# Half-array first scores, x_lo last, and copies of batch 0 first in a gated attention kernel

## What is computed

```python
qp = einsum('oc,bcn->bon', Wq, instance_norm(layernorm(x))) + bq
kp = einsum('oc,bcm->bom', Wk, instance_norm(ctx)) + bk
sp = einsum('oc,bcm->bom', Ws, ctx) + bs
attn = softmax(einsum('bcn,bcm->bnm', qp, kp), axis=-1)
mean = einsum('bnm,bvm->bvn', attn, sp)
std = sqrt(relu(einsum('bnm,bvm->bvn', attn, sp * sp) - mean * mean))
x = x + tanh(g_xattn) * (instance_norm(ctx) * std + mean)
x = x + tanh(g_ffn) * (layernorm(x) @ w.T)
```

## Time and profile before

| | |
|---|---|
| median of 3 runs | 191.2 us (191.08 to 192.58) |
| the profiled execution: own time | 191.17 us |
| the profiled execution: span | 189.4 us |
| TensorE busy | 168.2 us (89% of the span) |
| VectorE busy | 140.7 us (74%) |
| GpSimd busy | 133.9 us (71%) |
| ScalarE busy | 131.8 us (70%) |
| DMA queue of SyncE, share of 16 engines | 37.0% |

### The profile page before, as it was taken

How to read it: one execution, slowest core, us unless ns; L and a number is a source line. 1 busy time by engine, 2 the same in 40 slices (tenths; PEclk the granted TensorE clock), 3 DMA queues, 4 the chain that set the end, 5 groups by cost and what they waited for, 6 DMA issues and landing times.

```text
span 189.4 us, 2916 instructions
## 1 busy us (share of the span) xinstructions
PE 168.2 (89%) x816; PEld 104.7 (55%) x816; DVE 140.7 (74%) x321; ACT 131.8 (70%) x283; POOL 133.9 (71%) x155
## 2 busy tenths in 40 slices
PE   0349699999999999989998999899979889999993
PEld 0325455665556466545654565456435444888881
DVE  3877798679976967997699769994896753585641
ACT  2365766949796879759786968697779689626210
POOL 2225578538995899679969987998979999494100
PEclk9999999999999999999999999999999999999999
DMA  6248491477068427813680470064000000021312
GB/s 188 82 96 236 110 239 44 116 172 268 2 141 262 154 49 173 294 42 88 165 294 12 105 175 0 0 157 123 3 2 0 0 0 3 5 106 55 114 55 111
DMA packets 10880, 20.09 MB, mean 106 GB/s; under 512 B 1648, under 2 KB 1776, under 8 KB 10864
## 3 DMA queue, kind: packets, MB, share of 16 engines
q1 hardware_dynamic: 10864, 19.90, 37.0%
HBM read 9.67 MB, written 2.10 MB: 62 GB/s over the span
## 4 chain that ended last, share of the span: by engine, by line
PE 64%; DVE 15%; POOL 5%; issue 4%; ACT 4%; DMA 3%; SPq 2%; DVEq 0%; POOLq 0%; ACTq 0%
PE pv_bank L364 19%; PE score_bank L340 10%; PE turn_bank L351 10%; DVE neg_max L694 4%; PE score_bank L397 4%; PE score_bank L401 4%; PE score_bank L398 4%; POOL probs L889 3%; PE proj_bank L376 3%; PE proj_bank L322 3%; DMA params_sb<-in_params 2%; POOL x_lo L882 2%; ACT probs L492 2%; PE score_bank L387 2%; SPq L249 2%
## 5 line engine op out<-in xcount | busy, mean ns | idle before, releaser
L889 POOL TENSOR_SCALAR probs<-probs,rden 128x512 f32<-128x512 f32 x64 | 55.0, 859 | 19.4 <-DVE rden L700 19.1
L492 ACT ACTIVATE probs<-score_bank,neg_max 128x512 f32<-128x512 f32 x64 | 44.5, 696 | 24.2 <-DVE neg_max L694 23.9
L364 PE MATMUL pv_bank<-probs_t,values 128*128 128x512 f32 x120 | 60.2, 604 | 0.9 <-ACT VAR L509 0.6
L694 DVE TENSOR_REDUCE neg_max<-score_bank 128x1 f32<-128x512 f32 x64 | 43.4, 680 | 18.9 <-PE score_bank L340 18.8
L351 PEld LDWEIGHTS turn_bank<-ident,probs 128*128 128x128 f32 x256 | 29.4, 141 | 27.0 <-issue 22.4
L351 PE MATMUL turn_bank<-ident,probs 128*128 128x128 f32 x256 | 37.1, 277 | 4.3 <-ACT probs_t L500 2.9
L500 ACT COPY probs_t<-turn_bank 128x512 f32<-128x512 f32 x64 | 37.9, 591 | 1.2 <-PE turn_bank L351 1.0
L364 PEld LDWEIGHTS pv_bank<-probs_t,values 128*128 128x128 f32 x120 | 19.7, 190 | 13.0 <-issue 12.5
L340 PE MATMUL score_bank<-k_hi,q_hi 64*128 64x512 f32 x32 | 16.3, 509 | 2.8 <-DVE k_lo_swapped L776 2.5
L340 PE MATMUL score_bank<-k_hi_swapped,q_hi_swapped 64*128 64x512 f32 x32 | 16.3, 509 | 0.0
L397 PE MATMUL score_bank<-w_hi,yt_hi 128*128 128x512 f32 x32 | 13.6, 424 | 0.0
(11 more groups left out here) (105 smaller groups left out, 340.2 us busy)
## 6 DMA issues: line engine op xcount, KB each, us to landing
X<-in_x SPq DMA_DIRECT2D x8, 256.0 KB, 3.0
CTX<-in_context SPq DMA_DIRECT2D x8, 256.0 KB, 3.7
q_hi_swapped<-q_hi SPq DMA_DIRECT2D x16, 128.0 KB, 2.3
q_lo_swapped<-q_lo SPq DMA_DIRECT2D x16, 128.0 KB, 2.4
ctx_now<-in_context SPq DMA_DIRECT2D x8, 256.0 KB, 2.7
sz<-in_scales_zeros SPq DMA_DIRECT2D x4, 512.0 KB, 5.1
out<-result SPq DMA_DIRECT2D x8, 256.0 KB, 2.0
k_hi_swapped<-k_hi SPq DMA_DIRECT2D x15, 128.0 KB, 2.4
```

The costliest lines, as they stand in the source:

```text
L364: mm = pe.matmul(sums_bank(t, b)[:, :], values[:, i, b, :, :].rearrange("p a c -> p (a c)"), probs_t[b][:, i, :], start=(i == 0), stop=(i ...
L492: act.activation(probs[c % SBANKS][:, :], score_bank[c % SBANKS][:, :], ACT.Exp, bias=neg_max[:, c:c + 1], accum_out=den[:, c:c + 1]).then ...
L694: dve.tensor_reduce(neg_max[:, c:c + 1], score_bank[c % SBANKS][:, :], AX_X, ALU.max, negate=True).then_inc(max_done, 1)
L889: pool.tensor_scalar(probs[c % SBANKS][:, :], probs[c % SBANKS][:, :], rden[:, c:c + 1], 1.0, ALU.mult, ALU.mult).then_inc(probs_done, 1)
```

## The change

Five edits. (1) `project` issues the two products that read the hi part first and waits for the lo part only before the third. (2) A new function `first_scores(c)` makes the chunks 0 to 3 of tile 0 one after the other on the lower half of the array, where batch 0 lies, from q and k themselves; the shifted copies of batch 0 of tile 0 fall away on SyncE (two), ScalarE (one) and VectorE (one), and the counts of `swapped[0][0]` and of the wait in `maximum` follow. (3) VectorE runs the statistics of tile 1 after `keep_lo` of tile 0 instead of before. (4) SyncE issues the four copies of batch 0 of the next tile as each of q_hi, q_lo, k_hi, k_lo is ready, and the four of batch 1 after them. (5) In the start the context tile for the values is loaded before x and context of tile 2.

```diff
--- before.py
+++ after.py
@@ -262,28 +262,27 @@
             load(1, *first_loaded[1])
 
             sp.wait_ge(q_hi_done, 1)
-            swap(0, 0, swap_q_hi)
+            swap(0, 1, swap_q_hi)
             sp.wait_ge(q_lo_done, 1)
-            swap(0, 0, swap_q_lo)
+            swap(0, 1, swap_q_lo)
             sp.wait_ge(k_lo_done, 1)
-            swap(0, 1, swap_q_hi, swap_q_lo, swap_k_hi, swap_k_lo)
+            swap(0, 1, swap_k_hi, swap_k_lo)
+            sp.dma_start(ctx_now[:, :], dram_tile(context_tiles, 0)).then_inc(ctx_now_loaded, DMA)
             load(2, *first_loaded[2])
-            sp.dma_start(ctx_now[:, :], dram_tile(context_tiles, 0)).then_inc(ctx_now_loaded, DMA)
 
             def body(t):
 
                 if not has_next(t):
                     return
                 sp.wait_ge(q_hi_done, t + 2)
+                swap(t + 1, 0, swap_q_hi)
                 sp.wait_ge(q_lo_done, t + 2)
-                for b in range(2):
-                    swap(t + 1, b, swap_q_hi, swap_q_lo)
+                swap(t + 1, 0, swap_q_lo)
                 sp.wait_ge(k_hi_done, t + 2)
-                for b in range(2):
-                    swap(t + 1, b, swap_k_hi)
+                swap(t + 1, 0, swap_k_hi)
                 sp.wait_ge(k_lo_done, t + 2)
-                for b in range(2):
-                    swap(t + 1, b, swap_k_lo)
+                swap(t + 1, 0, swap_k_lo)
+                swap(t + 1, 1, swap_q_hi, swap_q_lo, swap_k_hi, swap_k_lo)
                 sp.wait_ge(s_done, t + 1)
                 sp.dma_start(ctx_now[:, :], dram_tile(context_tiles, t + 1)).then_inc(ctx_now_loaded, DMA)
 
@@ -318,16 +317,27 @@
                     (x_hi, x_lo, x_hi_done, x_lo_done, q_done), (c_hi, c_lo, c_hi_done, c_lo_done, k_done))[which]
                 into = bank_of(t, which)
                 pe.wait_ge(hi_done, t + 1)
+                pe.matmul(into[:, :], w_qk_hi[:, which, :], hi[:, :], start=True, stop=False)
+                pe.matmul(into[:, :], w_qk_lo[:, which, :], hi[:, :], start=False, stop=False)
                 pe.wait_ge(lo_done, t + 1)
-                pe.matmul(into[:, :], w_qk_hi[:, which, :], hi[:, :], start=True, stop=False)
-                pe.matmul(into[:, :], w_qk_hi[:, which, :], lo[:, :], start=False, stop=False)
-                pe.matmul(into[:, :], w_qk_lo[:, which, :], hi[:, :], start=False, stop=True).then_inc(done, 1)
+                pe.matmul(into[:, :], w_qk_hi[:, which, :], lo[:, :], start=False, stop=True).then_inc(done, 1)
+
+            def first_scores(c):
+
+                rows = slice(0, C)
+                if c == 0:
+                    pe.wait_ge(q_lo_done, 1)
+                    pe.wait_ge(k_lo_done, 1)
+                for step, (q_part, k_part) in enumerate(((q_hi, k_hi), (q_lo, k_hi), (q_hi, k_lo))):
+                    mm = pe.matmul(score_bank[c][:, :], q_part[0][rows, P * c:P * c + P], k_part[0][rows, :],
+                                   start=(step == 0), stop=(step == 2))
+                mm.then_inc(scores_done, 1)
 
             def scores(t, c):
 
                 b, p = c // JC, t % 2
                 if c % JC == 0:
-                    pe.wait_ge(swapped[b][p], SWAP * (t // 2 + 1))
+                    pe.wait_ge(swapped[b][p], SWAP * (t // 2 + (0 if (b, p) == (0, 0) else 1)))
                     pe.wait_ge(k_lo_done, t + 1)
                 if not (is_first(t) and c < SBANKS):
                     pe.wait_ge(exp_done, CHUNKS * t + c + 2 - SBANKS)
@@ -405,9 +415,8 @@
             pe.wait_ge(w_split, 1)
             project(0, 0)
             project(0, 1)
-            for c in range(0, SBANKS, 2):
-                scores(0, c)
-            pe.wait_ge(q_lo_done, 1)
+            for c in range(SBANKS):
+                first_scores(c)
             project(1, 0)
             pe.wait_ge(ident_ready, 1)
 
@@ -549,8 +558,6 @@
                 act.copy(part[:, :], whole).then_inc(part_done, 1)
             keep_hi(0, 0)
             keep_hi(0, 1)
-            act.wait_ge(k_hi_done, 1)
-            act.copy(k_hi_swapped[0][C:P, :], k_hi[0][0:C, :].bitcast(F32)).then_inc(swapped[0][0], DMA)
             act.preload_act_table_set("natural_log_exp_and_others")
             for c in range(AHEAD_E):
                 exponentials(0, c)
@@ -690,7 +697,7 @@
 
             def maximum(t, c):
 
-                dve.wait_ge(scores_done, CHUNKS * t + 2 * (c // 2) + 2)
+                dve.wait_ge(scores_done, CHUNKS * t + (c if is_first(t) and c < SBANKS else 2 * (c // 2) + 1) + 1)
                 dve.tensor_reduce(neg_max[:, c:c + 1], score_bank[c % SBANKS][:, :], AX_X, ALU.max,
                                   negate=True).then_inc(max_done, 1)
 
@@ -769,11 +776,9 @@
             dve.wait_ge(c_hi_done, 1)
             dve.tensor_tensor(c_lo[:, :], tile_of(CTX, 0), c_hi[:, :].bitcast(F32),
                               ALU.subtract).then_inc(c_lo_done, 1)
-            statistics(1)
             keep_lo(0, 0)
             keep_lo(0, 1)
-            dve.wait_ge(k_lo_done, 1)
-            dve.tensor_copy(k_lo_swapped[0][C:P, :], k_lo[0][0:C, :].bitcast(F32)).then_inc(swapped[0][0], DMA)
+            statistics(1)
             normalise(1, 0)
             dve.wait_ge(gates_ready, 1)
             for c in range(AHEAD_S):
```

## The result

| | before | changed |
|---|---|---|
| median | 191.45 us (191.08 to 192.58, 4 runs) | 193.69 us (193.25 to 194.35, 4 runs) |
| ratio, 95% interval | | 1.0109 (1.0056 to 1.0163) |
| profiled execution: own time, span | 191.17, 189.4 us | 194.35, 192.5 us |
| mean granted clock of TensorE | 1.00 | 0.961 |

The change makes the kernel slower by about 1.1%; the forecast was 190.9 us, the range ended at 191.9. The profiled execution is the slowest of the four; the others took 193.25 to 193.82 us, with a mean granted clock of 0.997 to 1.00, and what follows is read from the profiled one.

The account below looks back on a forecast made before the run. Bound by a sequence across all engines until 30 us, TensorE alone in tiles 1 and 2, then a VectorE-TensorE loop. Only the start's 0.25 us counted: 191.17 - 0.25 = 190.92, forecast 190.9 us, range 189.5 to 191.9.

Parts of the forecast that it names:

- First projection product: Tile 0: no longer waiting for x_lo, it starts at 6.84 instead of 7.75; the projections end 0.91 us earlier.
- first score product: Tile 0: without waiting for shifted copies it starts at 11.4 instead of 13.11, 1.7 us earlier.
- first maximum: Tile 0 on VectorE: starts between 14.9 and 15.0, where it stood (14.89).
- the moved statistics pay back a gain: Start, VectorE: tile 1's statistics behind k_lo pay back the projections' 0.9 us and the scores' 1.7 us.
- x_lo on GpSimd was covered: Tile 1: x_lo moves to about 15.1 to 16.4, its projection ends near 17, before q_hi at 17.89; cost nothing.
- The scores of tile 1 are released by no copy: Tile 1: scores start after the transposes at about 25.75 instead of 26.11, with 0.07 about 0.45 us sooner.
- Tiles 3 to 5: About 0.48 us of each x projection's wait is filled, but q_lo comes no sooner; gain taken as 0.
- rival A: Tiles 3 to 5: the x projection's 0.48 us counts three times, 1.44 us in all; time 189.5; chance 0.15.
- the last step of the sum: Tile 1: GpSimd's squared values limit the first weighing, 27.15 instead of 27.39; 0.24 of 0.45 us is kept.
- Tile 0 to tile 1: First maximum through tile 1's q_lo moves by s; the context projection starts at 19.98 + s, k_hi gains about 0.07 us.
- s: Shift of the first maximum in tile 0: +0.05 us (0 to +0.1).
- Rival B: Start: half-array products don't raise TensorE's pace, tile 1 runs slow until about 22.5, +1.4 at k_hi; 192.3 us; chance 0.10.

Follow-up runs that it names:

- the filled kernel: Changed kernel plus unread products: other array half beside first chunks, identity products at the start, around the first scores and in tile 7's pause; 190.11 us.
- the doubled products: Changed kernel with an unread second product on the other half of the array beside each of the twelve first score products; median 191.6 us, ratio 1.0014.
- the pauses filled: Changed kernel with five unread identity products: three before the first scores, one behind them, one behind tile 1's x projection; 191.27 us, ratio 0.9996.
- 14 products: Kernel before with 14 unread identity products ahead of the first projection: on 128 rows 191.12 us, on 64 rows 191.32 us.
- with pairs: Changed kernel with the second edit taken back, so six score pairs on both halves with their ScalarE and VectorE copies; 194.31 us, ratio 1.0133.

## Why the prediction was wrong

**Right, by its steps.** First projection product 6.82 (forecast 6.84), first score product 11.40 (11.4), first maximum 14.80 (14.9 to 15.0). That the moved statistics pay back a gain is confirmed from the other side, too: put back in the filled kernel, they give 1.1 us at the first maximum (13.95 to 12.85) and 0.9 in the time; without the filling it was not tried. q_hi of tile 1 was on time (17.79; before 17.89), so x_lo on GpSimd was covered. The scores of tile 1 are released by no copy. Tiles 3 to 5 gave nothing, q_lo took the place of x_lo as forecast, and the period of the projection product is still 18.1 us (89.89, 108.03, 126.16); rival A is false. Where the level is back in time, the last step of the sum holds as well: in the profile of the doubled products (191.04 us) the first weighing of values starts at 27.23, against 27.50 before; the forecast was 0.24 earlier.

**The step that failed** is "Tile 0 to tile 1": it let everything from the first maximum to the context projection move by s, with the durations that the rows of before show from 16.86 on. This holds only at the clock that those rows had. The context projection came at 20.88 instead of 19.98 + s, its three products took 0.43 to 0.57 each, and k_hi was 1.48 late instead of 0.07 early. Rival B had that price, +1.4 at k_hi, and the sign that I had named for it, products of 0.43 beyond 17.5 us, is the one that came (q_hi of tile 1 was not late, as B had it). But B ended too soon. It let the level return after k_hi; it stayed low until 27.4, and the transposes, the eight small products and the chunks 6 and 7 brought the 1.48 to 3.05.

**Why B had only 0.10.** I wrote against it that TensorE works longer without a gap than before, from 11.4 on. That took more busy time as a guarantee that the level rises and stays, and it is none here. The idle time before the scores did get shorter, 1.66 us instead of 2.46, and from 10 to 18 us TensorE is busy for 6.02 us, against 5.17 in the kernel before; the level fell all the same. The chunks were over soon after 14.31, while x_hi came 1.16 us later than before (14.45 instead of 13.29) and x_lo behind it, both held by the moved statistics, and the weighed probabilities came when they had come before; so part of the time won in front became idle time behind. That can have kept the level low; it didn't bring it down, for the fall at 13.7 came earlier. With the pauses filled the time (191.27, ratio 0.9996) lies in the forecast's range, but it can't be told from no change either.

**B's mechanism was half right.** Half an array does raise the level less than a whole one (14 products, 0.43 against 0.23 behind them). But in the changed kernel's profiles the level was up before the half chunks and fell among them, which B didn't have; with pairs a low stretch is there as well (194.31), and with the half array and filled pauses it isn't (191.27). What mix of work and idle time the level follows is not settled by these runs, so why it fell at 13.7 stays open, and so does why single runs of some versions lie 1 to 3 us above the others.

The Trainium skill, "TensorE: Matmul & The Clock Gate", in its section on HAM oscillation, says that idle gaps between bursts of matmuls bring the throttle back in the middle of a kernel. The trace agrees in kind: the fall in tile 7 came behind 1.36 us without work, and in the changed kernel the low stretch is gone once the pauses are filled. The waits in that section's example are longer than these; here the measured ones decide, and one of 1.35 us in the kernel before passed without a fall.

## What to carry to other kernels

Before you move a piece of TensorE's work earlier, ask when what follows it gets its inputs: if that doesn't move too, you have only moved the idle time. And ask at which clock the rows were taken that you shift: a stretch that falls to the lower level costs all the work behind it, here 3 us in the profiled execution. Where pauses can't be removed, some small products on the whole array in them are worth a trial. And an instruction moved off one path (the statistics off the way to q_lo) lands on another: find the first common consumer, and see whether it comes any sooner.

## What the runs showed of the hardware

- The page's clock row is no witness for the start: it shows 1.00 up to the first change that was recorded, also where products are 0.43 apart (6.82 to 9.12 in the changed kernel; up to 22.3 us with edit 2 alone, mean granted clock 1.0). The distance between starts is.
- The level can change at other moments with the same work in front of it: high at 11.40 in the changed kernel, still low at 11.35 with the doubled products, which had done the same up to there. This may be why runs of one kernel differ by up to 3.6 us (190.98 to 194.61 there); that was not shown.
- Behind a pause of 1.36 us in the last tile the level fell in one profile, which cost 1.7 us; with the pause filled, the spread of 189.97 to 192.41 shrank to 189.91 to 190.38 in seven runs of eight. In the kernel before, the same pause of 1.35 us passed without a fall in the profiled execution.
